# The order of VectorE's layer-norm moments and of its head divisions in the slot loop of a fused two-block transformer kernel

## The chip, the cores and the metric

The kernel runs on one core of a Trainium2 chip. A core has five engines with a queue each, which run side by side and each in its own order: TensorE (PE, matrix products), VectorE (DVE, elementwise work and reductions), ScalarE (ACT, activation functions and copies), GpSimd (POOL, elementwise work) and SyncE (SP, which here only starts transfers). Engines wait for one another, and an engine for itself, by counting semaphores. The metric is the time of one execution on the device in microseconds (us); lower is better.

## The reference, cut to what matters

The input is x, 64 sequences of 64 rows of 256 values, and a context of the same shape. Two blocks follow each other. The first is a decoder layer: self attention, cross attention to the context, and an MLP, each behind a layer norm. The second reads its result as latents: attention over the context and the latents together, then an RMS norm and an MLP.

```python
ln_out = layernorm(hidden_states, ln1_s, ln1_b)
q, k, v = jnp.split(ln_out @ w_qkv + b_qkv, 3, axis=-1)
x = hidden_states + merge_heads(attention(q, k, v, ltor_mask)) @ w_ao + b_ao
ln_out = layernorm(x, ln2_s, ln2_b)
q = ln_out @ w_q + b_q;  k, v = jnp.split(encoder_states @ w_kv + b_kv, 2, axis=-1)
x = x + merge_heads(attention(q, k, v, cross_mask)) @ w_co + b_co
ln_out = layernorm(x, ln3_s, ln3_b)
x = x + gelu(ln_out @ w1 + b1) @ w2 + b2
...
h = jnp.concatenate([context, x], axis=1)         # second block: x are the latents
q = x @ q_w + q_b;  k, v = split(h @ kv_w + kv_b)
a = softmax(where(mask, q @ k.T / DH, -inf)) @ v  # 16 heads of 16
a = a @ out_w + out_b + x
out = rmsnorm(a, postnorm_w)
result = gelu(out @ mlp_w1 + mlp_b1) @ mlp_w2 + mlp_b2 + x
```

A layer norm needs the mean and the variance of each row (the moments). Attention ends with a division of each head by the sum of its exponentials.

## The kernel before

Two sequences make a unit of 128 rows, and there are 32 units. Every unit goes through some 14 stages: self attention (names end in `self`), cross attention (`cross`), the first MLP (`mlp0`), attention of the latents over context and latents (`ctx`, `lat`), and the second MLP (`mlp1`). Products run in halves of f16 (a high and a low part); the parts are made by ACT or POOL (high) and DVE (low), stand in a pair, and are turned by a transfer that SP starts.

The order of the work is written out by hand, once for each engine. A prologue fills the pipeline. A loop over the slots t = 8 to 31 (line 1577 for DVE) then does one stage for each of several units: in slot t the cross attention of unit t-3, the first MLP of t-4, the latent scores of t-5, the latent heads of t-6, the second MLP of t-7 and t-8. An epilogue empties it. The code of a stage is a small function, called with a unit and a name. Its waits are counts of semaphores: `q.wait_ge(name, n)` holds the next instruction of this engine, and all behind it, until the count is n.

The functions that matter, on DVE:

- `moments` (line 1157): BN_STATS reads 256 values of each row into bn (L1165); BN_AGGREGATE makes mean and variance of them in mv (L1167) and waits for the first; then minus_mean and var (L1176, L1177), or for `mlp1` mean_square and var (L1170, L1173), which wait for the second. POOL's `root` (L2448, L2451) waits for var and makes rstd and shift; ACT's `normalize` (L1938) makes xn from them; POOL's `high_pair` (L2457) the high half; DVE's `low_pair` (L1186) the low half; then the transposing transfer and PE's products.
- `denominators` (L1273): the reciprocals over. `divided` (L1280): the heads, from PE's `mix` (L598) in PSUM and over. ACT's `heads_high` (L1952) copies their high half, DVE's `heads_low` (L1195) makes the low half and waits for it.
- `add_residual` (L1291): adds PE's projection (L470) to x or xb; this also sets the PSUM bank free. `masked` (L1231, L1238): the scores (L564) with the mask. `largest_score` (L1248), `largest_both` (L1254), `shifted` (L1267): maxima and the scores less the maximum; for the latents POOL shifts the context's part (L2505).

In ACT's queue a slot has, in this order, `normalize(t-3,"cross")`, `normalize(t-4,"mlp0")`, `values` twice, `heads_high(t-6,"lat")`, `q_bias_cross(t-3)` (L1972), the GELUs (L2017), and the exponentials (L2003).

Of the kernel before, what the change touches and what calls it, by code (L numbers as in the profile page):

```python
# [25 lines left out]
UNITS = B // BU  # L26
# [21 lines left out]
XHAT_UP, TOP = 11, 15  # L48
# [130 lines left out]
def build(nc, x_in, ctxT_in, mask_self_in, mask_cross_in, mask_keys_in, cols_in, rows_in, weights_in,  # L179
          out):  # L180
    with ExitStack() as ctx:
# [842 lines left out]
        def _(e):  # L1024
# [132 lines left out]
            def moments(u, t):  # L1157

                src, shrink = residual(t, u), 2.0 ** (-2 * XHAT_UP)
                steps, n = sem["moments_" + t], 4 * u  # L1160
# [5 lines left out]
                q.wait_ge("moments_" + t, n + 1)  # L1166
                e.bn_aggr(mv[t][:, :], bn[t][:, :]).then_inc(steps, 1)  # L1167
# [142 lines left out]
            moments(0, "self")  # L1310
            moments(1, "self")
            two_heads(0)
# [9 lines left out]
            moments(2, "self")  # L1322
            powers(0, "mid")
# [29 lines left out]
            moments(0, "cross")  # L1353
            bias_rows(0, "co")
            shifted(1, "self", 0)
            shifted(1, "self", 1)
            moments(3, "self")
            k_spread(2, "self", 0)
# [7 lines left out]
            moments(4, "self")  # L1366
            denominators(1, "self")
# [19 lines left out]
            moments(1, "cross")  # L1387
            powers(0, "xin")
# [16 lines left out]
            moments(5, "self")  # L1405
            add_residual(0, "cross")
            moments(0, "mlp0")
            masked(1, "cross", 0)
# [13 lines left out]
            moments(2, "cross")  # L1422
            shifted(1, "cross", 0)
            masked(4, "self", 0)
            moments(6, "self")
            masked(4, "self", 1)
# [26 lines left out]
            moments(1, "mlp0")  # L1453
            largest_score(2, "cross", 1)
# [9 lines left out]
            moments(3, "cross")  # L1464
            k_spread(3, "cross", 0)
# [14 lines left out]
            moments(4, "cross")  # L1480
            hidden_lo(1, "mlp0", 1)
# [19 lines left out]
            moments(2, "mlp0")  # L1501
            largest_score(3, "cross", 1)
# [25 lines left out]
            moments(3, "mlp0")  # L1528
            hidden_lo(2, "mlp0", 0)
            hidden_lo(2, "mlp0", 1)  # L1530
            add_residual(0, "lat")
            moments(0, "mlp1")
            low_pair(3, "mlp0")
# [6 lines left out]
            moments(7, "self")  # L1540
            lat_low(2)
# [1456 lines left out]
```

## Time and profile before

| | |
|---|---|
| time, median of 3 runs | 1089.6 us (1088.24 to 1089.82) |
| span of the profiled execution | 1086.8 us |
| its own time | not listed apart; the median is 2.8 us above its span |
| PE busy | 1004.1 us, 92% |
| DVE busy | 988.4 us, 91% |
| ACT busy | 849.4 us, 78% |
| POOL busy | 681.9 us, 63% |
| mean granted TensorE clock | 0.983 of full speed |

The span is the time from the first to the last instruction. Shares of busy time are averages over prologue, loop and epilogue. An engine's rows stand in the order of its queue, so a row that starts late holds up all behind it. A row of the timeline that waited names the engine that ended its wait in brackets; waits of an engine for itself carry no such note and show only as a later start.

### The profile page before, as it was taken

What the parts mean: (1) busy time and instruction counts of PE and PEld (TensorE: products, weight loads), DVE (VectorE), ACT (ScalarE), POOL (GpSimd) and SP (SyncE); (2) the same over time, 40 slices, a digit from 0 to 9 for tenths busy, and PEclk for the clock granted to TensorE, in tenths of its full rate; (3) what the DMA queues carried; (4) which work ended last, traced back from release to release, by engine and by line L of the source; (5) the groups of instructions that cost most, each with busy time, mean ns of one, the idle gap of its engine ahead of it and who ended that gap; (6) DMA issues with size and microseconds to landing.
All of it is one profiled execution on the core that took longest, in us unless ns stands there. A gap on an engine that the chain in (4) does not pass through costs nothing.

```text
span 1086.8 us, 46478 instructions
## 1 busy us (share of the span) xinstructions
PE 1004.1 (92%) x19180; PEld 890.8 (82%) x19180; DVE 988.4 (91%) x2328; ACT 849.4 (78%) x1905; POOL 681.9 (63%) x909
## 2 busy tenths in 40 slices
PE   6776989999999999999999999999999999998997
PEld 5665778888888888888888888888888888886786
DVE  4989897999999999999999999999999999988763
ACT  3446789887888888888788888878888888786894
POOL 3777575666666667666667676666676676655221
PEclk9879999999999999999999999999999999999999
DMA  8843112222322222222222222222222222311111
GB/s 275 280 114 74 42 39 41 44 45 58 59 49 51 52 57 43 49 54 58 58 49 45 57 47 48 50 58 58 49 49 54 56 44 49 61 37 37 31 37 36
DMA packets 169700, 67.70 MB, mean 62 GB/s; under 512 B 151184, under 2 KB 167312, under 8 KB 168464
## 3 DMA queue, kind: packets, MB, share of 16 engines
q1 hardware_dynamic: 169488, 64.72, 26.1%
q8 instruction: 152, 2.49, 1.0%
q14 instruction: 60, 0.49, 0.2%
HBM read 26.93 MB, written 4.19 MB: 29 GB/s over the span
## 4 chain that ended last, share of the span: by engine, by line
PE 37%; ACT 26%; DVE 20%; issue 11%; POOL 4%; DMA 2%; SPq 0%; ACTq 0%; POOLq 0%; DVEq 0%
PE psum L457 9%; PE psum L598 7%; PE psum L630 7%; ACT staging L2017 7%; PE psum L470 6%; ACT hid_mlp L2017 6%; PE psum L564 3%; ACT L2003 3%; PE psum L584 3%; DVE mx_lat L1248 3%; ACT L2017 2%; ACT probT_self L2003 2%; DVE late L1267 2%; DVE mx_ctx L1254 2%; DMA turned_mlp<-pair_mlp 1%
## 5 line engine op out<-in xcount | busy, mean ns | idle before, releaser
L2499 POOL TENSOR_TENSOR prob_self<-prob_self,add_self 128x512 f32<-128x512 f32 x64 | 86.8, 1376 | 66.1 <-DVE prob_self L1238 63.4
L2499 POOL TENSOR_TENSOR prob_cross<-prob_cross,add_cross 128x512 f32<-128x512 f32 x64 | 94.5, 1495 | 52.9 <-DVE prob_cross L1238 52.9
L2505 POOL TENSOR_TENSOR late<-late,mx_ctx 128x512 f32<-128x512 f32 x64 | 67.3, 1053 | 86.6 <-DVE mx_ctx L1254 84.1
L2017 ACT ACTIVATE hid_mlp<-psum,folded,undo_in 128x128 f32<-128x128 f32 x256 | 95.6, 455 | 6.9 <-PE psum L457 6.4
L2017 ACT ACTIVATE staging<-psum,cols,undo_in 128x128 f32<-128x128 f32 x256 | 97.4, 481 | 3.3 <-PE psum L457 3.1
L457 PE MATMUL psum<-turned_mlp,hi_n 128*128 128x128 f16 x1024 | 94.2, 221 | 1.6 <-DVE late L1267 1.0
L630 PE MATMUL psum<-hi_n,staging 128*128 128x256 f16 x512 | 94.3, 273 | 1.5 <-DVE staging L1297 1.5
L457 PE MATMUL psum<-turned_mlp,hi_m 128*128 128x128 f16 x1024 | 93.4, 220 | 0.6 <-DMA turned_mlp<-pair_mlp 0.5
L630 PE MATMUL psum<-hi_m,parts_mlp 128*128 128x256 f16 x512 | 89.9, 273 | 1.2 <-DVE xb L1291 0.9
L457 PE MATMUL psum<-turned_mlp,lo_n 128*128 128x128 f16 x512 | 90.3, 221 | 0.0
L457 PE MATMUL psum<-turned_mlp,lo_m 128*128 128x128 f16 x512 | 89.6, 220 | 0.0
L457 PEld LDWEIGHTS psum<-turned_mlp,hi_m 128*128 128x128 f16 x1024 | 77.8, 98 | 7.3 <-issue 5.6
L457 PEld LDWEIGHTS psum<-turned_mlp,hi_n 128*128 128x128 f16 x1024 | 78.9, 99 | 4.1 <-issue 1.4
L2448 POOL TENSOR_TENSOR rstd_mlp<-var_mlp,minus_half 128x1 f32<-128x1 f32 x64 | 38.0, 593 | 60.8 <-DVE var_mlp L1173 59.9
L2476 POOL TENSOR_TENSOR xb<-x,rows 128x256 f32<-128x256 f32 x96 | 72.1, 752 | 5.9 <-DVE x L1307 3.0
L2003 ACT ACTIVATE late<-psum 128x512 f32<-128x512 f32 x128 | 69.7, 596 | 6.6 <-PE psum L584 6.4
L630 PE MATMUL psum<-lo_n,staging 128*128 128x256 f16 x256 | 69.8, 273 | 0.0
L630 PE MATMUL psum<-lo_m,parts_mlp 128*128 128x256 f16 x256 | 69.8, 273 | 0.0
L598 PE MATMUL psum<-val_ctx,late 128*64 128x34 f32 x1024 | 62.2, 225 | 0.8 <-ACT late L2003 0.7
L598 PE MATMUL psum<-val_lat,late 128*64 128x34 f32 x1024 | 61.5, 224 | 0.0
L584 PEld LDWEIGHTS psum<-ident,late 64*128 64x128 f32 x1024 | 35.8, 140 | 30.5 <-DVE late L1267 27.4
L584 PE MATMUL psum<-ident,late 64*128 64x64 f32 x1024 | 39.9, 227 | 22.1 <-DVE late L1267 20.7
(265 smaller groups left out, 3850.0 us busy)
## 6 DMA issues: line engine op xcount, KB each, us to landing
xin<-in_x SPq DMA_DIRECT2D x32, 128.0 KB, 2.2
late<-in_ctxT SPq DMA_DIRECT2D x4, 1024.0 KB, 5.7
ctxT<-in_ctxT SPq DMA_DIRECT2D x32, 128.0 KB, 2.0
late<-in_x SPq DMA_DIRECT2D x4, 1024.0 KB, 5.6
out<-xb SPq DMA_DIRECT2D x32, 128.0 KB, 1.9
staging<-in_w_m SPq DMA_DIRECT2D x2, 1024.0 KB, 7.2
staging<-in_w_n SPq DMA_DIRECT2D x2, 1024.0 KB, 5.2
mask<-in_mask_cross SPq DMA_DIRECT2D x32, 32.0 KB, 2.0
```

The lines of the kernel that those rows point to most:

```text
L457: last = e.matmul(out_ap, wt[name][:, k, c:c + P], xs[:, k, :], start=(n == 0), stop=(n == 3 * KH - 1))
L470: last = e.matmul(ps[:, 0:H], xs[:, k, :], wt[name][:, k, c:c + H], start=(n == 0), stop=(n == 3 * KH - 1))
L564: last = e.matmul(ps[here, h * HC * S:(h + 1) * HC * S], qT["lat" if t == "ctx" else t][rows_of, h, here], spread[t][rows_of, h, :, here], ...
L584: last = e.transpose(bank[in_bank["prob_turn", t, a, u]][:, n * S:(n + 1) * S], prob[t][h][here, j * P:(j + 1) * P], ident[here, here])
L598: last = e.matmul(ps[S * a:S * a + S, p * VW:(p + 1) * VW], probT[s][a][:, j, :], val[s][:, a, p, :], start=(n == 0), stop=(n == len(sets) ...
L630: last = e.matmul(ps[:, 0:H], a, wt, start=(g == 0 and n == 0), stop=(g == 1 and n == 11))
L2003: e.activation(probT[t][a][:, :, :], src, ACT.Exp).then_inc(sem["probT_" + t], 1)
L2017: last = e.activation(hid[t][g][:, j * P:(j + 1) * P], ps[:, j * P:(j + 1) * P], ACT.Gelu_apprx_tanh, bias=b1[:, 4 * g + j:4 * g + j + 1], ...
L2448: e.tensor_tensor(rstd[t][:, :], var[t][:, :], minus_half[:, :], ALU.pow).then_inc(sem["rstd_" + t], 1)
L2476: e.tensor_tensor(o[:, :], a[:, :], row, ALU.add).then_inc(sem["plus_bias_" + t], 1)
L2499: e.tensor_tensor(ch, ch, over_heads(a[:, :]), ALU.add).then_inc(sem["added_" + t], 1)
L2505: e.tensor_tensor(ch, ch, over_keys(max_of("ctx", h)), ALU.subtract).then_inc(sem["shifted_ctx"], 1)
```

## The change

`moments` becomes three calls: `moments` (BN_STATS), `aggregate` (BN_AGGREGATE) and `variance` (the rest). In prologue and epilogue the three calls stand one behind the other, so the order there is as before. In the slot loop other calls stand between them. The division of the heads stands one call behind the reciprocals: `largest_score` or `largest_both` goes ahead of it, and for the latent heads both `masked` calls. The statistics have one wait more, for the count of the unit before. The other engines' orders are not touched.

```diff
             def moments(u, t):
-                src, shrink = residual(t, u), 2.0 ** (-2 * XHAT_UP)
-                steps, n = sem["moments_" + t], 4 * u
+                src, steps = residual(t, u), sem["moments_" + t]
+                q.wait_ge("moments_" + t, 4 * u)
...
                 e.bn_stats(bn[t][:, :], src[:, :]).then_inc(steps, 1)
-                q.wait_ge("moments_" + t, n + 1)
-                e.bn_aggr(mv[t][:, :], bn[t][:, :]).then_inc(steps, 1)
+
+            @of_unit
+            def aggregate(u, t):
+
+                q.wait_ge("moments_" + t, 4 * u + 1)
+                e.bn_aggr(mv[t][:, :], bn[t][:, :]).then_inc(sem["moments_" + t], 1)
+
+            @of_unit
+            def variance(u, t):
+
+                shrink, steps, n = 2.0 ** (-2 * XHAT_UP), sem["moments_" + t], 4 * u
                 q.wait_ge("moments_" + t, n + 2)
...
                 moments(t - 7, "mlp1")
                 k_spread(t - 2, "self", 0)
+                aggregate(t - 7, "mlp1")
                 add_residual(t - 3, "self")
+                variance(t - 7, "mlp1")
                 moments(t - 3, "cross")
                 hidden_lo(t - 8, "mlp1", 0)
+                aggregate(t - 3, "cross")
                 add_residual(t - 4, "cross")
+                variance(t - 3, "cross")
                 moments(t - 4, "mlp0")
                 masked(t - 5, "ctx", 0)
+                aggregate(t - 4, "mlp0")
                 low_pair(t - 7, "mlp1")
+                variance(t - 4, "mlp0")
                 low_pair(t - 3, "cross")
...
                 moments(t, "self")
                 k_spread(t - 3, "cross", 0)
+                aggregate(t, "self")
                 denominators(t - 6, "lat")
+                variance(t, "self")
                 masked(t - 2, "self", 0)
+                masked(t - 2, "self", 1)
                 divided(t - 6, "lat")
-                masked(t - 2, "self", 1)
...
                 denominators(t - 2, "self")
+                largest_score(t - 5, "lat", 0)
                 divided(t - 2, "self")
-                largest_score(t - 5, "lat", 0)
                 heads_low(t - 2, "self")
                 denominators(t - 3, "cross")
+                largest_both(t - 5, 0)
                 divided(t - 3, "cross")
-                largest_both(t - 5, 0)
                 largest_score(t - 5, "lat", 1)
```

Three places show what moves on DVE; the line numbers of the changed kernel are 4 to 9 higher. The first is the head of a slot, from the residual of the cross attention (x) on; bn_mlp and mv_mlp are the moments of the first MLP, late the masked scores of the context. Before:

```order
L1291 SCALAR_TENSOR_TENSOR x<-psum,undo,xb 128x256
L1165 BN_STATS bn_mlp<-x 128x6
L1167 BN_AGGR mv_mlp<-bn_mlp 128x2
L1176 TENSOR_SCALAR minus_mean_mlp<-mv_mlp 128x1
L1177 TENSOR_SCALAR var_mlp<-mv_mlp 128x1
L1231 TENSOR_TENSOR late<-psum,keys_mask 128x512
L1183 SCALAR_TENSOR_TENSOR pair_mlp<-xb,rstd_mlp,pair_mlp 128x256
L1186 TENSOR_TENSOR pair_cross<-xn_cross,pair_cross 128x256
```

The same place after the change:

```order
L1300 SCALAR_TENSOR_TENSOR x<-psum,undo,xb 128x256
L1185 TENSOR_SCALAR minus_mean_cross<-mv_cross 128x1
L1186 TENSOR_SCALAR var_cross<-mv_cross 128x1
L1165 BN_STATS bn_mlp<-x 128x6
L1240 TENSOR_TENSOR late<-psum,keys_mask 128x512
L1171 BN_AGGR mv_mlp<-bn_mlp 128x2
L1192 SCALAR_TENSOR_TENSOR pair_mlp<-xb,rstd_mlp,pair_mlp 128x256
L1185 TENSOR_SCALAR minus_mean_mlp<-mv_mlp 128x1
L1186 TENSOR_SCALAR var_mlp<-mv_mlp 128x1
L1195 TENSOR_TENSOR pair_cross<-xn_cross,pair_cross 128x256
```

The last two steps of the cross moments are now behind the residual, and the aggregate of the MLP moments stands behind the mask, its variance behind pair_mlp (the low half of the second MLP).

The second place is the division of the latent heads (heads_lat) in the middle of a slot. Before:

```order
L1273 RECIPROCAL over_lat<-psum 128x16
L1238 TENSOR_TENSOR prob_self<-psum,mask_self 128x512
L1280 TENSOR_TENSOR heads_lat<-psum,over_lat 128x256
L1238 TENSOR_TENSOR prob_self<-psum,mask_self 128x512
L1213 SCALAR_TENSOR_TENSOR spread_cross<-psum,down_of_two_cross,bias_of_two_cross 128x2x128
L1195 TENSOR_TENSOR heads_pair_lat<-heads_lat,heads_pair_lat 128x256
```

The same place after the change:

```order
L1282 RECIPROCAL over_lat<-psum 128x16
L1185 TENSOR_SCALAR minus_mean_self<-mv_self 128x1
L1186 TENSOR_SCALAR var_self<-mv_self 128x1
L1247 TENSOR_TENSOR prob_self<-psum,mask_self 128x512 x2
L1289 TENSOR_TENSOR heads_lat<-psum,over_lat 128x256
L1222 SCALAR_TENSOR_TENSOR spread_cross<-psum,down_of_two_cross,bias_of_two_cross 128x2x128
L1204 TENSOR_TENSOR heads_pair_lat<-heads_lat,heads_pair_lat 128x256
```

Both masked scores (prob_self) and the end of the moments of x stand now ahead of heads_lat.

The third place is the end of a slot, from the reciprocals of the self heads (over_self) on. Before:

```order
L1273 RECIPROCAL over_self<-psum 128x16
L1280 TENSOR_TENSOR heads_self<-psum,over_self 128x256
L1248 TENSOR_REDUCE mx_lat<-psum 128x8
L1195 TENSOR_TENSOR heads_pair_self<-heads_self,heads_pair_self 128x256
L1273 RECIPROCAL over_cross<-psum 128x16
L1280 TENSOR_TENSOR heads_cross<-psum,over_cross 128x256
L1254 TENSOR_TENSOR mx_ctx<-mx_ctx,mx_lat 128x8
L1248 TENSOR_REDUCE mx_lat<-psum 128x8
L1195 TENSOR_TENSOR heads_pair_cross<-heads_cross,heads_pair_cross 128x256
L1254 TENSOR_TENSOR mx_ctx<-mx_ctx,mx_lat 128x8
```

The same place after the change:

```order
L1282 RECIPROCAL over_self<-psum 128x16
L1257 TENSOR_REDUCE mx_lat<-psum 128x8
L1289 TENSOR_TENSOR heads_self<-psum,over_self 128x256
L1204 TENSOR_TENSOR heads_pair_self<-heads_self,heads_pair_self 128x256
L1282 RECIPROCAL over_cross<-psum 128x16
L1263 TENSOR_TENSOR mx_ctx<-mx_ctx,mx_lat 128x8
L1289 TENSOR_TENSOR heads_cross<-psum,over_cross 128x256
L1257 TENSOR_REDUCE mx_lat<-psum 128x8
L1204 TENSOR_TENSOR heads_pair_cross<-heads_cross,heads_pair_cross 128x256
L1263 TENSOR_TENSOR mx_ctx<-mx_ctx,mx_lat 128x8
```

heads_pair_self follows heads_self directly now, and the first mx_ctx follows over_cross directly.

## Rows read from the trace of the kernel before

**Rows 1.** The page, part 1: busy us, share, instructions of each engine.

```profile
PE 1004.1 (92%) x19180; PEld 890.8 (82%) x19180; DVE 988.4 (91%) x2328; ACT 849.4 (78%) x1905; POOL 681.9 (63%) x909
```

**Rows 2.** Timeline of DVE: start us, us, engine, line, op, names; the loop's ends.

```profile
189.21 0.41 DVE L1165 BATCH_NORM_STATS2 bn_mlp<-xb 128x6 f32<-128x256 f32 x1
...
899.06 0.41 DVE L1165 BATCH_NORM_STATS2 bn_mlp<-xb 128x6 f32<-128x256 f32 x1
```

**Rows 3.** Waits, 189 to 899: who for whom, us in total, times, longest.

```profile
PE psum L584 <- DVE late L1267: 18.0, 23, 0.8
```

**Rows 4.** Chain that ended last, 640 to 700: start us, us, what.

```profile
663.12 0.68 PE psum L457 x12
...
663.83 0.02 ACT q_cross L1972
...
664.65 1.28 ACT L2017
...
674.32 1.09 ACT probT_self L2003 x2
...
675.46 1.15 PE psum L598 x32
...
676.63 0.27 DVE over_self L1273
```

**Rows 5.** Timeline of DVE, head of the slot that starts at 652.24.

```profile
652.24 0.41 DVE L1165 BATCH_NORM_STATS2 bn_mlp<-xb 128x6 f32<-128x256 f32 x1
652.69 0.18 DVE L1167 BATCH_NORM_AGGREGATE mv_mlp<-bn_mlp 128x2 f32<-128x6 f32 x1
...
655.69 0.48 DVE L1291 SCALAR_TENSOR_TENSOR x<-psum,undo,xb 128x256 f32<-128x256 f32 x1
...
656.96 0.14 DVE L1177 TENSOR_SCALAR var_mlp<-mv_mlp 128x1 f32<-128x1 f32 x1
657.11 0.69 DVE L1231 TENSOR_TENSOR late<-psum,keys_mask 128x512 f32<-128x512 f32 x1
657.72 0.48 DVE L1183 SCALAR_TENSOR_TENSOR pair_mlp<-xb,rstd_mlp,pair_mlp 128x256 f16<-128x256 f32 x1
...
659.77 0.43 DVE L1186 TENSOR_TENSOR pair_mlp<-xn_mlp,pair_mlp 128x256 f16<-128x256 f32 x1 [0.25 <-POOL pair_mlp L2457]
```

**Rows 6.** Timeline of PE, the same slot.

```profile
655.27 0.38 PE L470 MATMUL psum<-lo_out,heads_turned_cross 128*128 128x256 f16 x2
...
656.32 0.70 PE L564 MATMUL psum<-spread_ctx,q_lat 32*64 32x128 f32 x32
```

**Rows 7.** Timeline of POOL, the same slot.

```profile
657.56 0.55 POOL L2448 TENSOR_TENSOR rstd_mlp<-var_mlp,minus_half 128x1 f32<-128x1 f32 x1
```

**Rows 8.** Timeline of DVE, the division of the latent heads.

```profile
662.68 0.41 DVE L1280 TENSOR_TENSOR heads_lat<-psum,over_lat 128x256 f32<-128x256 f32 x1
```

**Rows 9.** Timeline of ACT, behind that division.

```profile
663.13 0.41 ACT L1952 CAST heads_pair_lat<-heads_lat 128x256 f16<-128x256 f32 x1 [0.92 <-DVE heads_lat L1280]
```

**Rows 10.** Timeline of PE, end of the slot.

```profile
676.52 0.69 PE L564 MATMUL psum<-spread_lat,q_lat 32*64 32x128 f32 x32
```

**Rows 11.** Timeline of DVE, end of the slot.

```profile
677.33 0.69 DVE L1248 TENSOR_REDUCE mx_lat<-psum 128x8 f32<-128x512 f32 x1
...
678.32 0.26 DVE L1273 RECIPROCAL over_cross<-psum 128x16 f32<-128x16 f32 x1
...
678.95 0.16 DVE L1254 TENSOR_TENSOR mx_ctx<-mx_ctx,mx_lat 128x8 f32<-128x8 f32 x1
...
680.43 0.68 DVE L1254 TENSOR_TENSOR mx_ctx<-mx_ctx,mx_lat 128x8 f32<-128x8 f32 x1
...
681.04 1.27 DVE L1267 TENSOR_TENSOR late<-psum,mx_ctx 128x512 f32<-128x512 f32 x2
...
683.02 0.41 DVE L1165 BATCH_NORM_STATS2 bn_mlp<-xb 128x6 f32<-128x256 f32 x1
```

**Rows 12.** Timeline of POOL, end of the slot.

```profile
680.18 0.91 POOL L2476 TENSOR_TENSOR x<-x,rows 128x256 f32<-128x256 f32 x1
```

More of the change, by code:

```diff
@@ L1310, in _ @@
             moments(0, "self")
+            aggregate(0, "self")
+            variance(0, "self")
             moments(1, "self")
+            aggregate(1, "self")
+            variance(1, "self")
             two_heads(0)
@@ L1322, in _ @@
             moments(2, "self")
+            aggregate(2, "self")
+            variance(2, "self")
             powers(0, "mid")
@@ L1353, in _ @@
             moments(0, "cross")
+            aggregate(0, "cross")
+            variance(0, "cross")
             bias_rows(0, "co")
@@ L1357, in _ @@
             moments(3, "self")
+            aggregate(3, "self")
+            variance(3, "self")
             k_spread(2, "self", 0)
@@ L1366, in _ @@
             moments(4, "self")
+            aggregate(4, "self")
+            variance(4, "self")
             denominators(1, "self")
@@ L1387, in _ @@
             moments(1, "cross")
+            aggregate(1, "cross")
+            variance(1, "cross")
             powers(0, "xin")
@@ L1405, in _ @@
             moments(5, "self")
+            aggregate(5, "self")
+            variance(5, "self")
             add_residual(0, "cross")
             moments(0, "mlp0")
+            aggregate(0, "mlp0")
+            variance(0, "mlp0")
             masked(1, "cross", 0)
@@ L1422, in _ @@
             moments(2, "cross")
+            aggregate(2, "cross")
+            variance(2, "cross")
             shifted(1, "cross", 0)
@@ L1425, in _ @@
             moments(6, "self")
+            aggregate(6, "self")
+            variance(6, "self")
             masked(4, "self", 1)
@@ L1453, in _ @@
             moments(1, "mlp0")
+            aggregate(1, "mlp0")
+            variance(1, "mlp0")
             largest_score(2, "cross", 1)
@@ L1464, in _ @@
             moments(3, "cross")
+            aggregate(3, "cross")
+            variance(3, "cross")
             k_spread(3, "cross", 0)
@@ L1480, in _ @@
             moments(4, "cross")
+            aggregate(4, "cross")
+            variance(4, "cross")
             hidden_lo(1, "mlp0", 1)
@@ L1501, in _ @@
             moments(2, "mlp0")
+            aggregate(2, "mlp0")
+            variance(2, "mlp0")
             largest_score(3, "cross", 1)
@@ L1528, in _ @@
             moments(3, "mlp0")
+            aggregate(3, "mlp0")
+            variance(3, "mlp0")
             hidden_lo(2, "mlp0", 0)
@@ L1532, in _ @@
             moments(0, "mlp1")
+            aggregate(0, "mlp1")
+            variance(0, "mlp1")
             low_pair(3, "mlp0")
@@ L1540, in _ @@
             moments(7, "self")
+            aggregate(7, "self")
+            variance(7, "self")
             lat_low(2)
@@ L1642, in _ @@
             moments(UNITS - 3, "cross")
+            aggregate(UNITS - 3, "cross")
+            variance(UNITS - 3, "cross")
             add_residual(UNITS - 4, "cross")
@@ L1704, in _ @@
             moments(UNITS - 2, "cross")
+            aggregate(UNITS - 2, "cross")
+            variance(UNITS - 2, "cross")
             add_residual(UNITS - 3, "cross")
@@ L1749, in _ @@
             moments(UNITS - 1, "cross")
+            aggregate(UNITS - 1, "cross")
+            variance(UNITS - 1, "cross")
             k_spread(UNITS - 1, "cross", 0)
@@ L1793, in _ @@
             moments(UNITS - 1, "mlp0")
+            aggregate(UNITS - 1, "mlp0")
+            variance(UNITS - 1, "mlp0")
             add_mlp(UNITS - 6, "mlp1")
```

20 lines of the change are left out of this document (added).

## The prediction

> **What bounds the kernel now.** The page's busy line comes first: PE 92% and DVE 91% of the span, so neither has room by itself [rows 1]. The timeline then gives the slot's length. The loop's 24 slots each begin at DVE's statistics of the block xb; the first starts at 189.21, the last at 899.06, so a slot lasts (899.06 - 189.21) / 23 = 30.86 us, and 24 of them are 741 us of the 1086.8 [rows 2]. The waits say who waits in the loop: PE waits for DVE's second shift of the latent scores, 18.0 us in 23 slots, 0.78 us in each [rows 3]. The chain that ended last says where one slot's length comes from [rows 4]. PE works from that shift up to the query product of the cross attention (until 663.12 + 0.68 = 663.80). ACT takes it up at 663.83 and is then never idle: table load at 664.65, GELUs, second table load, exponentials of the self scores from 674.32. PE's mix starts at 675.46, DVE's reciprocal at 676.63, and DVE carries the chain to the next shift (from 681.04 [rows 11]). So a slot is three pieces: PE up to 663.80, ACT up to the mix, DVE's tail. Time counts only if it moves one of them.
>
> **What the change takes away, and why I price it at nothing.** The statistics take 0.41, but the aggregate that waits for them starts 0.45 later [rows 5]. A row that waits for nothing starts 0.08 before the one ahead of it ends (the mask at 657.11 takes 0.69, the next row starts at 657.72) [rows 5]. A self-wait thus costs 0.45 - 0.33 = 0.12, that behind the aggregate about as much. Four moments lose two each, two divisions one each: about 10 x 0.12 = 1.2 us of DVE a slot. At the head of the slot, however, DVE soon waits for others. Its add of the cross residual at 655.69 follows PE's projection, which ends at 655.27 + 0.38 = 655.65; the mask at 657.11 follows PE's scores, which wait for that add and end at 656.32 + 0.70 = 657.02 [rows 5, 6]. Neither can start earlier because DVE arrives earlier. The saving becomes idle time there, and the same fixed points now stand between the pieces of the moments.
>
> The Trainium skill bears on this: "VectorE: DVE Perf Modes", section The DRAIN you can't avoid, says in my words that a semaphore between two chained VectorE operations costs nothing extra. The trace disagrees for these short ones (0.45 against 0.33). By that rule the saving would be zero instead of 1.2 us a slot; my sum is the same by both.
>
> **What it moves: the head of the slot.** DVE's variance of the MLP block ends now at 656.96 + 0.14 = 657.10 [rows 5]. After the change the statistics stand ahead of the mask, but the aggregate behind it, and the variance behind the low half of the other MLP block. From the fixed mask at 657.11: aggregate 657.72, low half 0.18 - 0.08 later at 657.82, minus_mean 0.48 - 0.08 later at 658.22, variance 0.07 later at 658.29, end 658.43. That is 1.33 us later. Behind it hangs a chain over three engines: POOL's root, ACT's normalisation, POOL's high half, DVE's low half at 659.77, for which DVE already waits 0.25 us now; there is no slack to swallow anything [rows 5]. POOL's root starts today at 657.56, when POOL comes free [rows 7]; afterwards at 658.43 + 0.04 = 658.47, so 0.91 later. The chain from it to DVE's low half is 659.77 - 657.56 = 2.21 as before: low half at 660.68. DVE has nothing else it may do (its rows are in order) and idles.
>
> Then the division of the latent heads. Today it starts 662.68 - 659.77 = 2.91 behind the low half [rows 5, 8]. Now both masks stand ahead of it instead of one (+0.60, the distance 657.72 - 657.11), and two self-waits of the moments of x are gone (-0.23): 660.68 + 2.91 + 0.37 = 663.96. ACT's copy of the heads stands in ACT's queue ahead of the bias of the cross queries; today it starts 0.04 behind the division (662.68 + 0.41 = 663.09 against 663.13) and ends at 663.54, in time for 663.83 [rows 4, 8, 9]. Afterwards it ends at 663.96 + 0.41 + 0.04 + 0.41 = 664.82, so the bias starts at 664.84 instead of 663.83: +1.01 us. Everything behind it on ACT is back to back, so the mix and DVE's reciprocal come 1.01 later too. PE has its own delay of about 0.9 from the transposed low half, which stays beneath this; nothing else on POOL or SP is moved.
>
> **What it moves: the tail.** I count from the reciprocal of the self heads, R = 676.63. The reduction of the latent scores is now ahead of the division, but its scores leave PE at 676.52 + 0.69 = 677.21 = R + 0.58 [rows 10], so it starts at R + 0.62, hardly ahead of today's 677.33 = R + 0.70 [rows 11]. Division at R + 1.23, end 0.42 later at R + 1.65. Behind the division now stands directly the low half of the self heads, which needs ACT's copy (0.04 + 0.41, as in [rows 9]): R + 2.10, start R + 2.13. Until now the reduction covered that copy. The reciprocal of the cross heads follows 0.33 later at R + 2.46; today it is at 678.32 = R + 1.69, so 0.77 are lost. Part comes back: the maximum of both (mx_ctx) now stands directly behind that reciprocal, 0.17 instead of 678.95 - 678.32 = 0.63. It starts at R + 2.63 against R + 2.32: +0.31. From it to the shift I keep today's 681.04 - 678.95 = 2.09, because that stretch is set by POOL: the second maximum takes 0.68 where the first takes 0.16, and ends (681.11) with POOL's 0.91 us row at 681.09 [rows 11, 12], which is started by the first maximum through the row ahead of it. Tail: +0.31.
>
> The Trainium skill, "SBUF — State Buffer", section SBUF: two separate sides, says that VectorE and GpSimd take a shared port pair as an exclusive lock, whoever starts first holding it for the whole instruction. The 0.68 against 0.16 agrees. By it the tail keeps its 2.09; without it the stretch would shrink by up to 0.52, and the tail would be -0.21 instead of +0.31.
>
> **Sum.** 1.01 + 0.31 = 1.32 us on the slot shown, which lasts 683.02 - 652.24 = 30.78 [rows 5, 11]: 32.10. Against the mean of 30.86 that is +1.24, as the short waits that make some slots longer are covered by the new one; 24 x 1.24 = 29.8. Prologue and epilogue keep their order (the three calls stand together there) and get 0. The profiled execution spans 1086.8, and the median of the runs is 1089.6, 2.8 more for what lies around it. 1086.8 + 29.8 + 2.8 = 1119.4 us.
>
> Bounds. The head is at least the extra mask, 0.60 (the low half as today), less the 0.29 that ACT's copy has to spare (663.83 - 663.54): 0.3. It is at most 1.5, if POOL's later root meets DVE rows that stretch it as they do the maximum (0.52). I take 1.01, since its points are rows. The tail is at least -0.21 and at most 0.77, if nothing comes back. All ends together would give 24 x 0.1 to 24 x 2.2; for the range I take half of each side's way, since the ends of the two terms don't hang together.
>
> **The rivals.** (1) DVE is the engine that bounds, and its 1.2 us a slot reach PE's 0.78 us of waiting [rows 3]: 24 x 0.78 = 18.7 faster, 1070.9. For it: the 91%. It decides once the head's variance comes no later than POOL can use it, that is by 657.56; against it stand 1.33 us of lateness where DVE waits already. Chance 0.07. (2) The self-waits were beneath other engines' time and the delays are covered as well: 1089.6. Chance 0.03. (3) The low half is not late, because the mask at 657.11 comes earlier than I think, and only the tail's 0.31 counts: 24 x 0.31 = 7.4, 1097.0. Against it: PE's scores, which wait for the add. Chance 0.10. (4) Both terms at their long ends (+1.5 and +0.77), against it that POOL has pauses between: 24 x 2.2 = 53, up to 1142. Chance 0.08.
>
> **How the numbers follow.** My forecast, 1119.4, has 0.72. The range 1096 to 1131 takes in (3) and the halves of the bounds, and leaves out (1), (2) and most of (4), somewhat under 0.2 together. A difference of 0.2% (2.2 us) is about what a measurement of this kernel can tell from none. Faster 0.07, same 0.04 (case 2 and a weak tail), slower 0.89.
>
> **What would show it.** In the profile after: a slot of about 32.1 us; DVE idle about 1 us before pair_mlp<-xn_mlp with POOL as releaser; ACT's q_cross no longer released by PE but starting right behind heads_pair_lat, whose wait for DVE heads_lat grows; a new wait of some 0.5 us of DVE heads_pair_self for ACT; POOL's two rows at the end as long as before; PE's waits grow in the middle of the slot (hidden or k_lat products), not only at the transposes of the latent scores. I would be wrong if DVE's idle before pair_mlp stays at 0.25 us, if q_cross is still released by PE, or if the slot gets shorter than 30.8.

## The result

| | before | after |
|---|---|---|
| median | 1089.7 us | 1130.6 us |
| its runs | 1088.24 to 1090.49 | 1128.95 to 1132.33 |
| profiled span | 1086.8 us | 1127.5 us |
| slot, mean of the loop | 30.86 us | 32.48 us |

The ratio is 1.0373, 95% interval 1.0355 to 1.0392: the changed kernel is 3.7% slower, 40.8 us. The forecast was 1119.4 us in a range of 1096 to 1131; the measured median lies 0.4 us inside its upper end. Of the 40.7 us between the spans, the loop holds 24 x (32.48 - 30.86) = 38.9.

### The profile page after: what moved, and what is told of

It reads as the page before. It is cut to its first block, busy times and chain, and to the rows that moved or that the text cites. A ratio compares the mean times of both kernels' runs of the same rounds, so it can differ in the third digit from the quotient of the medians.

```text
span 1127.5 us, 46602 instructions
## 1 busy us (share of the span) xinstructions
PE 1017.8 (90%) x19180; PEld 891.0 (79%) x19180; DVE 984.2 (87%) x2328; ACT 854.8 (76%) x1905; POOL 675.4 (60%) x909
## 4 chain that ended last, share of the span: by engine, by line
PE 42%; DVE 25%; issue 15%; ACT 11%; POOL 7%; DMA 1%; ACTq 0%; POOLq 0%; SPq 0%; DVEq 0%
PE psum L457 16%; PE psum L630 7%; PE psum L584 6%; PE psum L470 4%; PE psum L564 4%; PE psum L598 3%; DVE late L1276 2%; DVE mx_self L1257 2%; DVE staging L1306 2%; DVE prob_self L1247 2%; DVE mx_ctx L1263 2%; ACT xn_mlp L2019 1%; POOL rstd_mlp L2529 1%; DVE mx_lat L1257 1%; ACT xn_cross L2019 1%
## 5 line engine op out<-in xcount | busy, mean ns | idle before, releaser
L2580 POOL TENSOR_TENSOR prob_self<-prob_self,add_self 128x512 f32<-128x512 f32 x64 | 82.0, 1300 | 60.6 <-DVE prob_self L1247 57.8
L598 PE MATMUL psum<-val_ctx,late 128*64 128x34 f32 x1024 | 62.2, 225 | 0.7 <-ACT late L2084 0.6
L598 PE MATMUL psum<-val_lat,late 128*64 128x34 f32 x1024 | 61.6, 224 | 0.0
L630 PEld LDWEIGHTS psum<-hi_n,staging 128*128 128x128 f16 x512 | 50.0, 98 | 12.5 <-issue 4.5
L630 PEld LDWEIGHTS psum<-hi_m,parts_mlp 128*128 128x128 f16 x512 | 50.1, 98 | 11.8 <-DVE parts_mlp L1306 6.1
```

The costliest lines, as they stand in the source:

```text
L598: last = e.matmul(ps[S * a:S * a + S, p * VW:(p + 1) * VW], probT[s][a][:, j, :], val[s][:, a, p, :], start=(n == 0), stop=(n == len(sets) ...
L630: last = e.matmul(ps[:, 0:H], a, wt, start=(g == 0 and n == 0), stop=(g == 1 and n == 11))
L2580: e.tensor_tensor(ch, ch, over_heads(a[:, :]), ALU.add).then_inc(sem["added_" + t], 1)
```

## The profile after

The busy line, against [rows 1]. Each engine does about as much as before in a longer span; no busy time explains 40 us.

```profile
PE 1017.8 (90%) x19180; PEld 891.0 (79%) x19180; DVE 984.2 (87%) x2328; ACT 854.8 (76%) x1905; POOL 675.4 (60%) x909
```

The loop's ends on DVE, against [rows 2]: (936.23 - 189.18) / 23 = 32.48 us.

```profile
189.18 0.41 DVE L1165 BATCH_NORM_STATS2 bn_mlp<-xb 128x6 f32<-128x256 f32 x1
...
936.23 0.41 DVE L1165 BATCH_NORM_STATS2 bn_mlp<-xb 128x6 f32<-128x256 f32 x1
```

The waits of PE and DVE over the whole span that matter here (engine, what waits, for whom: us in total, times, longest). The first, fourth, fifth and last are new. The second stood at 20.7 in 27 over the whole span before, of which [rows 3] show the loop's part.

```profile
PE psum L564 <- DVE xb L1316: 18.2, 24, 0.8
...
PE psum L584 <- DVE late L1276: 15.1, 27, 1.0
DVE pair_mlp L1195 <- POOL pair_mlp L2538: 14.6, 27, 1.7
...
DVE mx_lat L1257 <- PE psum L564: 11.6, 27, 0.8
DVE heads_pair_self L1204 <- ACT heads_pair_self L2033: 11.3, 24, 0.5
PE psum L564 <- ACT val_ctx L2076: 11.0, 24, 0.6
```

PE now waits with two of its scores (L564) in each of the 24 slots, once for ACT's val_ctx and once for DVE's add of the MLP product (L1316). By the kernel's bank numbers each of the two reads a PSUM bank that those scores are then written into. Times below are also given from the slot's start, here 643.76.

DVE's timeline, head of that slot; it answers to [rows 5, 8].

```profile
643.76 0.41 DVE L1165 BATCH_NORM_STATS2 bn_mlp<-xb 128x6 f32<-128x256 f32 x1
...
648.63 0.69 DVE L1240 TENSOR_TENSOR late<-psum,keys_mask 128x512 f32<-128x512 f32 x1 [0.41 <-PE psum L564]
...
649.76 0.14 DVE L1186 TENSOR_SCALAR var_mlp<-mv_mlp 128x1 f32<-128x1 f32 x1
...
652.01 0.42 DVE L1195 TENSOR_TENSOR pair_mlp<-xn_mlp,pair_mlp 128x256 f16<-128x256 f32 x1 [0.52 <-POOL pair_mlp L2538]
...
655.26 0.42 DVE L1289 TENSOR_TENSOR heads_lat<-psum,over_lat 128x256 f32<-128x256 f32 x1
...
656.15 1.47 DVE L1204 TENSOR_TENSOR heads_pair_lat<-heads_lat,heads_pair_lat 128x256 f16<-128x256 f32 x1
...
658.14 0.47 DVE L1316 SCALAR_TENSOR_TENSOR xb<-psum,undo_out,x 128x256 f32<-128x256 f32 x1
```

The mask stands at 4.87, as before (657.11 - 652.24), waiting 0.41 for PE. The variance is at 6.00 instead of 4.72, the low half at 8.25 instead of 7.53, the division at 11.50 instead of 10.44. Then a row that nobody had in view: heads_pair_lat takes 1.47 us. In the kernel before the same row takes 0.41:

```profile
664.00 0.41 DVE L1195 TENSOR_TENSOR heads_pair_lat<-heads_lat,heads_pair_lat 128x256 f16<-128x256 f32 x1
```

POOL's timeline, first before, then after. Two rows of prob_self stand in one line of 2.70 or 2.50 us.

```profile
662.85 2.70 POOL L2499 TENSOR_TENSOR prob_self<-prob_self,add_self 128x512 f32<-128x512 f32 x2 [2.34 <-DVE prob_self L1238]
```

```profile
647.89 0.55 POOL L2529 TENSOR_TENSOR rstd_cross<-var_cross,minus_half 128x1 f32<-128x1 f32 x1 [1.24 <-DVE var_cross L1186]
...
649.47 0.56 POOL L2538 CAST pair_cross<-xn_cross 128x256 f16<-128x256 f32 x1 [0.76 <-ACT xn_cross L2019]
650.00 0.54 POOL L2529 TENSOR_TENSOR rstd_mlp<-var_mlp,minus_half 128x1 f32<-128x1 f32 x1
650.62 0.19 POOL L2532 TENSOR_TENSOR shift_mlp<-minus_mean_mlp,rstd_mlp 128x1 f32<-128x1 f32 x1
...
654.84 2.50 POOL L2580 TENSOR_TENSOR prob_self<-prob_self,add_self 128x512 f32<-128x512 f32 x2 [2.10 <-DVE prob_self L1247]
```

Before, heads_pair_lat begins 1.15 us into POOL's pair (664.00 - 662.85), ahead of the second row. After, it begins 1.31 us in (656.15 - 654.84), when POOL, at half of its 2.50 us, has just begun its second; it ends at 657.62, and POOL's pair ends at 657.34. The DVE row is held until POOL's is done. Before, POOL's first row, of 1.28 us, had 0.13 left when the DVE row began, and the DVE row ended 0.29 behind it; after, the second row had 1.19 left, and the DVE row ended 0.28 behind it. So in both kernels it ends about 0.28 behind the POOL row that runs when it begins, and 1.19 + 0.28 makes the 1.47.

ACT's timeline, against [rows 9] and the q_cross of [rows 4].

```profile
650.91 0.60 ACT L2019 ACTIVATE xn_mlp<-x,shift_mlp,rstd_mlp 128x256 f32<-128x256 f32 x1 [1.50 <-POOL shift_mlp L2532]
651.42 1.50 ACT L2076 ACTIVATE val_ctx<-psum,undo 64x128 f32<-64x128 f32 x4
...
655.71 0.40 ACT L2033 CAST heads_pair_lat<-heads_lat 128x256 f16<-128x256 f32 x1 [1.27 <-DVE heads_lat L1289]
656.14 0.81 ACT L2053 ACTIVATE q_cross<-psum,folded,down_q 128x128 f32<-128x128 f32 x2
```

The query bias q_cross follows ACT's copy without a wait and starts at 12.38 instead of 11.59, so 0.79 later. PE's two rows of scores are later by 0.52 and by 1.51. First the rows before, at 8.77 and 13.49 of their slot (start 652.24), then after, at 9.29 and 15.00:

```profile
661.01 0.69 PE L564 MATMUL psum<-spread_self,q_self 32*64 32x128 f32 x32
...
665.73 0.69 PE L564 MATMUL psum<-spread_cross,q_cross 32*64 32x128 f32 x32
```

```profile
653.05 0.89 PE L564 MATMUL psum<-spread_self,q_self 32*64 32x128 f32 x32 [0.46 <-ACT val_ctx L2076]
...
658.76 0.70 PE L564 MATMUL psum<-spread_cross,q_cross 32*64 32x128 f32 x32 [0.45 <-DVE xb L1316]
```

The chain of waits in this slot (start, us, what) runs through the held row. The 1.36 us stand as "issue", since no semaphore explains them; read beside POOL's line they are the hold.

```profile
655.71 0.41 ACT heads_pair_lat L2033
...
656.15 0.04 DVE heads_pair_lat L1204
656.19 1.36 issue
657.55 0.67 DVE mx_self L1257
658.22 0.40 DVE xb L1316
...
658.76 0.70 PE psum L564 x32
659.45 2.79 PE psum L457 x48
...
668.33 1.12 PE psum L598 x32
669.45 0.71 PE psum L564 x32
```

From the cross scores on the chain is PE's own work, up to the mix of the self heads (L598) that ends at 669.45, just ahead of DVE's reciprocal at 669.50. In the loop PE's idle time between these scores and that reciprocal has a median of 0.21 us a slot before, a wait for ACT's probT_self ahead of the mix, and of 0.00 after. So the middle piece of the slot, which ACT bounded before, is bounded by PE here: the reciprocal follows the cross scores by 10.74 us, against 10.90 before.

The tail on DVE, against [rows 11]; R, the start of the reciprocal of the self heads, is 669.50.

```profile
669.50 0.26 DVE L1282 RECIPROCAL over_self<-psum 128x16 f32<-128x16 f32 x1
670.18 0.69 DVE L1257 TENSOR_REDUCE mx_lat<-psum 128x8 f32<-128x512 f32 x1 [0.42 <-PE psum L564]
...
671.67 0.42 DVE L1204 TENSOR_TENSOR heads_pair_self<-heads_self,heads_pair_self 128x256 f16<-128x256 f32 x1 [0.47 <-ACT heads_pair_self L2033]
...
672.18 0.10 DVE L1263 TENSOR_TENSOR mx_ctx<-mx_ctx,mx_lat 128x8 f32<-128x8 f32 x1
...
674.23 1.27 DVE L1276 TENSOR_TENSOR late<-psum,mx_ctx 128x512 f32<-128x512 f32 x2
```

From R to the shift 674.23 - 669.50 = 4.73 us, against 4.41. POOL's row beneath the end, against [rows 12], is as long as it was:

```profile
673.37 0.91 POOL L2557 TENSOR_TENSOR x<-x,rows 128x256 f32<-128x256 f32 x1
```

## The experiments

The theory: the time comes from three places, and each can be taken back alone. (M) The spread moments make POOL's roots, ACT's mlp0 normalisation and so val_ctx late, and PE's self scores wait. (L) The lat division behind both masks puts heads_pair_lat beneath POOL's second prob_self row. (T) The tail is 0.32 longer. The rivals: the added semaphore wait itself costs; or ACT's q_cross alone carries the head; or the parts don't add.

The first seven columns of numbers are medians over 21 slots of the loop, from each kernel's timeline, in us: from the slot's start the low half (pair_mlp), PE's self scores, heads_pair_lat (with its own duration), PE's cross scores, R; then the way from R to the shift. The last is the mean slot.

| kernel | pair_mlp | self scores | heads_pair_lat | takes | cross scores | R | R to shift | slot |
|---|---|---|---|---|---|---|---|---|
| before | 7.53 | 8.77 | 11.76 | 0.42 | 13.49 | 24.39 | 4.41 | 30.85 |
| after | 8.24 | 9.29 | 12.39 | 1.47 | 14.99 | 25.73 | 4.73 | 32.46 |
| a_wait_only | 7.58 | 8.83 | 11.81 | 0.41 | 13.55 | 24.44 | 4.40 | 30.86 |
| b_divisions_only | 7.53 | 8.77 | 11.92 | 1.46 | 14.52 | 25.26 | 4.72 | 31.98 |
| c_moments_only | 8.24 | 9.29 | 12.22 | 0.41 | 14.02 | 24.91 | 4.40 | 31.39 |
| d_lat_division_back | 8.25 | 9.29 | 12.23 | 0.42 | 14.02 | 24.91 | 4.73 | 31.70 |
| f_low_half_later | 8.24 | 9.29 | 13.77 | 0.41 | 14.09 | 25.31 | 4.61 | 31.93 |
| h_self_division_back | 8.25 | 9.29 | 12.39 | 1.46 | 14.99 | 25.73 | 3.90 | 31.66 |
| g_maximum_first | 7.53 | 8.77 | 11.75 | 0.42 | 13.49 | 24.39 | 3.90 | 30.36 |
| m_values_first | 9.50 | 8.77 | 13.48 | 0.41 | 15.16 | 26.05 | 4.41 | 32.45 |
| n_one_group_back | 8.18 | 9.23 | 12.16 | 0.42 | 13.95 | 24.86 | 4.40 | 31.37 |
| p_one_group_only | 8.40 | 9.45 | 12.63 | 0.42 | 14.32 | 25.22 | 4.40 | 31.68 |
| q_both_orders | 8.18 | 9.22 | 12.16 | 0.42 | 13.95 | 24.85 | 3.89 | 30.83 |
| r_two_groups_back | 7.72 | 8.96 | 11.70 | 0.41 | 13.68 | 24.71 | 3.77 | 30.50 |

**a_wait_only.** The new functions with their wait, nothing between the calls, divisions as before.

```diff
+                aggregate(t - 4, "mlp0")
+                variance(t - 4, "mlp0")
                 masked(t - 5, "ctx", 0)
```

> The moments are split into three calls that stand one behind the other everywhere, the divisions stand as before; what is left of the change is the one wait more on each statistics row. Theory M (the change costs by what it moves, nothing by its waits): within 0.2% of before, 1089.6. Rival W (the added wait costs sequencer time on each of 4 statistics a slot, up to 0.05 us each in the chain): 24 x 0.2 = 5 us slower, 1094.5.

Measured 1090.8 us, ratio 1.001 (0.9994 to 1.0027). The added wait costs nothing that can be measured; all of the 3.7% is order.

**b_divisions_only and c_moments_only.** Each half of the change alone.

```diff
                 masked(t - 2, "self", 0)
-                divided(t - 6, "lat")
                 masked(t - 2, "self", 1)
+                divided(t - 6, "lat")
```

> Only the three divisions are moved; the moments stay together as before. Theory L (DVE's low half of the latent heads, a row with two SBUF inputs, now starts just behind POOL's second row of the self scores and is held for its length): heads_pair_lat takes about 1.47 us instead of 0.42, the score of the cross attention starts about 1.05 us later, the tail costs 0.2 to 0.3: slot +1.2, 1118. Rival H (no such hold; only ACT's copy is 0.33 late and the tail 0.31): heads_pair_lat 0.42 us, slot +0.64, 1105. Rival M1 (the cost sits in the moments alone): 1090.

> Only the moments are spread in the loop; the three divisions stand as before. The low half of the first MLP comes 0.7 us later, the division of the latent heads then about 0.5 us later (10.93 us into the slot instead of 10.44), one self-wait group being saved; ACT's bias of the cross queries +0.2 to +0.3. Theory L: heads_pair_lat starts just ahead of POOL's second row as before and takes 0.42: slot +0.3, 1097. Rival (the moments carry the whole head term by themselves): slot +0.8 to +1.0, 1109 to 1114.

Measured: divisions 1115.9 us, ratio 1.0237 (1.0207 to 1.0267); moments 1103.3 us, ratio 1.0125 (1.0087 to 1.0164), against 1089.6 for the kernel before. They add within these intervals: 26.3 + 13.7 = 40.0 of 40.8. The time of the divisions was 2 us under what was expected. That of the moments fell between the theory's 1097 and the rival's 1109: they cost 0.54 us a slot where 0.3 was expected, because PE's late self scores were not in the theory. The long heads_pair_lat comes with the divisions (1.46) and not with the moments (0.41):

```profile
650.28 1.46 DVE L1195 TENSOR_TENSOR heads_pair_lat<-heads_lat,heads_pair_lat 128x256 f16<-128x256 f32 x1
```

```profile
671.43 0.41 DVE L1204 TENSOR_TENSOR heads_pair_lat<-heads_lat,heads_pair_lat 128x256 f16<-128x256 f32 x1
```

The delays of PE's scores split alike: self scores +0.52 from the moments and 0 from the divisions, cross scores +0.53 and +1.03, which makes 1.56 against the 1.50 seen together. In c the chain of waits runs from the late variance of cross over POOL's cast and its root of mlp0, ACT's normalisation and val_ctx to PE's self scores and on to q_cross, which comes 0.52 later (12.11 against 11.59), as R does. Its step from ACT to PE (start, us, what; slot start 659.21):

```profile
667.98 0.38 ACT val_ctx L2076
...
668.50 0.70 PE psum L564 x32
```

**d_lat_division_back.** The kernel after, with the lat division between the masks again (the reverse of the diff above).

> The changed kernel with only the division of the latent heads back between the two masks. Theory L: heads_pair_lat goes back to 0.42 us, PE's cross scores stop waiting for DVE's add; what is left is the moments' part (13.7 us measured alone) and the tail's 0.16 to 0.3 a slot: 1107 to 1111. Rival (the division of the latent heads is a small part, under 5 us of the 26 that the divisions cost together): 1125 or more.

Measured 1111.1 us, ratio 1.0202 (1.0186 to 1.0218): 19.5 us back, at the upper edge of what was expected. The row takes 0.42, the cross scores come at 14.02 as with the moments alone, and the wait for L1316 is gone.

**f_low_half_later.** The kernel after, with the low half of the lat heads behind three rows, so that it starts when POOL has finished its pair.

```diff
-                heads_low(t - 6, "lat")
                 largest_score(t - 2, "self", 0)
                 add_mlp(t - 8, "mlp1")
                 k_spread(t - 5, "lat", 0)
+                heads_low(t - 6, "lat")
```

> The changed kernel with heads_low of the latent heads moved three calls later, behind largest_score, add_mlp and k_spread, so that DVE doesn't meet POOL's row with it and add_mlp frees its PSUM bank earlier. Theory L: add_mlp no longer waits behind the held row, PE's cross scores start about 0.5 to 1 us earlier and the slot is bound by ACT's late copy (+0.8) and the tail (+0.25): slot 31.9, 1115. Rival (the hold is only a symptom; the slot is set by ACT's copy and the tail anyway): no change against the changed kernel, 1130.

Measured 1117.2 us, ratio 1.0262 (1.0213 to 1.031): 13.4 us back. The same row, later still, takes 0.41, so it is the meeting with POOL's row that makes it long. The cross scores return to 14.09, and ACT bounds the middle piece again. R keeps 0.40 more than in d, and the traces say why (medians). ACT's q_cross follows the late copy without a wait, at 12.38 against 12.12 in d, and PE's mix waits 0.42 for ACT's exponentials instead of 0.22 and starts at 24.02 instead of 23.74: 0.28. The other 0.12 is another held row: DVE's pair_lat, just ahead of the reciprocal, begins as POOL passes from one row to the next (xb to ctx_lo, in the median slot 0.04 behind it) and takes 0.99, ending 0.28 behind POOL's row; in d it takes 0.47.

**h_self_division_back.** The kernel after, with the self division ahead of the reduction again.

```diff
+                divided(t - 2, "self")
                 largest_score(t - 5, "lat", 0)
-                divided(t - 2, "self")
```

> The changed kernel with the division of the self heads back ahead of the reduction of the latent scores, so that this covers ACT's copy again. Theory T: heads_pair_self loses its wait of 0.47 us and mx_lat its wait of 0.42; the shift comes 0.75 to 0.87 earlier: 1110 to 1112. Rival (the slot is set by the head alone and the tail's wait is idle time anyway): 1130.5.

Measured 1109.4 us, ratio 1.0187 (1.017 to 1.0204). That is 0.6 us under the range. The head is untouched (R at 25.73), the tail falls from 4.73 to 3.90. So the tail's +0.32 is a loss of 0.83 by the self division and a gain of 0.51 by the cross division.

**g_maximum_first.** The kernel before, with only the edit that gains.

```diff
-                divided(t - 3, "cross")
                 largest_both(t - 5, 0)
+                divided(t - 3, "cross")
```

> The kernel before with one swap: largest_both (mx_ctx) directly behind the reciprocals of the cross heads, ahead of their division; nothing else of the change. Theory T (the stretch from the first mx_ctx to the shift is set by POOL's rows and only moves with its start): mx_ctx starts 0.46 us earlier, the shift too, slot 30.4, 24 x 0.46 = 11 us faster, 1078.6. Rival P (PE is not free for the transposes earlier, or the shift doesn't follow): within 0.2% of before, 1089.6.

Measured 1078.0 us, ratio 0.9898 (0.9877 to 0.9919): faster than both kernels, by one move out of the changed kernel's seven. DVE's tail, then POOL's:

```profile
670.99 0.10 DVE L1254 TENSOR_TENSOR mx_ctx<-mx_ctx,mx_lat 128x8 f32<-128x8 f32 x1
...
672.05 0.45 DVE L1195 TENSOR_TENSOR heads_pair_cross<-heads_cross,heads_pair_cross 128x256 f16<-128x256 f32 x1
```

```profile
671.18 1.04 POOL L2505 TENSOR_TENSOR late<-late,mx_ctx 128x512 f32<-128x512 f32 x1 [1.08 <-DVE mx_ctx L1254]
```

The maximum releases POOL's late row 0.50 us earlier (26.44 of the slot against 26.94 before, medians), and that row is nearly over when heads_pair_cross starts, which takes 0.45. In c_moments_only, whose tail is that of before, it takes 0.88 beneath the same POOL row.

**m_values_first.** c_moments_only, with ACT's val_ctx ahead of the mlp0 normalisation, to free PE's bank early.

```diff
+                values(t - 5, "ctx")
                 normalize(t - 4, "mlp0")
-                values(t - 5, "ctx")
```

> Moments spread, divisions as before (the kernel that took 1103.3), and in ACT's queue the values of the context ahead of the normalisation for the first MLP. Theory V (the moments cost through PE: its self scores wait for a PSUM bank that ACT's val_ctx frees, and val_ctx stands in ACT's queue behind the late xn_mlp): the wait of 0.46 us before the self scores goes, slot 31.0, 1092 to 1095. Rival C (the cost comes over ACT's copy of the latent heads or over the transposed low half): no change, 1103.

A miss: 1129.1 us, ratio 1.0366 (1.0348 to 1.0385). The waits of its whole span:

```profile
DVE pair_mlp L1195 <- POOL pair_mlp L2538: 44.7, 27, 1.8
...
PE psum L630 <- DVE staging L1306: 30.0, 27, 1.2
ACT val_ctx L2076 <- PE psum L598: 29.2, 24, 1.2
```

PE's self scores are on time (8.77). But val_ctx itself waits 1.2 us for PE's mix, and the normalisation stood behind it in ACT's queue: the low half comes at 9.50, DVE idles 1.8 us, and PE waits 1.2 us for the staging behind it. So this run shows that the bank can be freed in time, and that the low half then takes over; it does not by itself show what the bank's wait costs in c. For that stand c's chain of waits and run r below.

**n_one_group_back and p_one_group_only.** Which of the four spread moments costs: c with mlp0's calls together again, and a with only mlp0's spread.

```diff
                 moments(t - 4, "mlp0")
-                masked(t - 5, "ctx", 0)
                 aggregate(t - 4, "mlp0")
-                low_pair(t - 7, "mlp1")
                 variance(t - 4, "mlp0")
+                masked(t - 5, "ctx", 0)
+                low_pair(t - 7, "mlp1")
```

> The moments of three residuals stay spread over the slot (mlp1, cross, self); only those of mlp0, whose result the path through GpSimd waits for, stand together again ahead of masked(ctx, 0). Divisions as in the kernel before. Theory: the whole cost of the spread moments is that mlp0's variance comes 1.3 us later and DVE's pair_mlp with it; with these together pair_mlp starts no later than before and the slot is back at 30.9 us or a little under: 1082 to 1091 us. Rival: the spread costs wherever it is made (x of self waits for PE, ACT's normalizations come late): 1096 to 1103 us, near the kernel in which all four are spread.

> The complement: the three calls follow each other directly for self, cross and mlp1, and only mlp0's are spread, over masked(ctx, 0) and the low half of mlp1. Divisions as in the kernel before. Theory: pair_mlp about 0.7 us later, at offset 8.2 to 8.5 us of the slot, nothing saved elsewhere: 1101 to 1108 us, as the kernel with all four spread or slower by the self-waits that it does not save. Rival: no more than 1095 us, since the cost lies in the other groups.

Measured 1103.7 us, ratio 1.0118 (1.0095 to 1.014), and 1111.2 us, ratio 1.0189 (1.0163 to 1.0216). The first expectation fell: with mlp0's variance back at 4.8, nothing is won. The second came out 3 us above its range of 1101 to 1108, and 8 us above c. So once mlp0's variance is late, spreading the other three groups as well wins 0.29 us a slot (31.39 against 31.68); by what was not taken apart. POOL's rows of n (slot start 629.95), then of p (633.54):

```profile
634.09 0.55 POOL L2529 TENSOR_TENSOR rstd_cross<-var_cross,minus_half 128x1 f32<-128x1 f32 x1 [1.23 <-DVE var_cross L1186]
...
635.67 0.50 POOL L2538 CAST pair_cross<-xn_cross 128x256 f16<-128x256 f32 x1 [0.76 <-ACT xn_cross L2019]
636.13 0.55 POOL L2529 TENSOR_TENSOR rstd_mlp<-var_mlp,minus_half 128x1 f32<-128x1 f32 x1
```

```profile
639.83 0.66 POOL L2529 TENSOR_TENSOR rstd_mlp<-var_mlp,minus_half 128x1 f32<-128x1 f32 x1 [0.85 <-DVE var_mlp L1186]
```

In n the mlp0 root waits for nobody: it stands behind POOL's cast for cross, which is late because the variance of cross came at 3.91 instead of 2.72. It starts at 6.18. In p it waits for mlp0's variance and starts at 6.29. Before it starts at 5.32. Two delays meet in one queue, and either is enough.

**q_both_orders and r_two_groups_back.** g with the moments spread as in n; then cross's calls together too, so that only those of mlp1 and self are spread.

```diff
                 moments(t - 3, "cross")
-                hidden_lo(t - 8, "mlp1", 0)
                 aggregate(t - 3, "cross")
-                add_residual(t - 4, "cross")
                 variance(t - 3, "cross")
+                hidden_lo(t - 8, "mlp1", 0)
+                add_residual(t - 4, "cross")
```

> The order that the findings point to: the moments of mlp1, cross and self spread, mlp0's together, and the first largest-score call ahead of the division of cross, the other two divisions as in the kernel before. Theory: the gain of the maximum first (11.7 us) and that of the spread (0 to 8 us) add: 1070 to 1079 us. Rival: TensorE bounds both and VectorE's saved time is worth nothing: 1078 us.

> As the kernel in which both orders are changed (maximum first; moments of mlp1, cross and self spread; 1088.8 us), but cross's three calls stand together again too, so that only mlp1's and self's are spread. Reading of the last three traces: GpSimd takes the root of cross, its cast and the root of mlp0 in one row, and either variance late (cross at 3.93 instead of 2.74, or mlp0 at 6.02 instead of 4.74) makes it late by the same 0.7 us, so putting one back gave nothing. Theory: with both back, mlp0's normalization on ScalarE starts at 6.4 to 6.6 instead of 7.1, TensorE's self scores wait under 0.2 us for val_ctx, and the time is that of the maximum first alone or less, by the self-waits saved: 1072 to 1080 us. Rival: the wait of add_residual(self) for TensorE (0.58 us at offset 1.5) or mlp1's root 1.2 us later costs by itself: 1084 to 1089 us.

Measured 1088.8 us, ratio 0.9995 (0.998 to 1.001), and 1082.8 us, ratio 0.9949 (0.993 to 0.9968). The first was wrong for n's reason. The second confirms the path but missed its range by 3 us: ACT's normalisation starts at 6.62 (6.43 before), the self scores at 8.96 without a wait. Along g, r, q the self scores stand at 8.77, 8.96, 9.22 and the slot at 30.36, 30.50, 30.83. The 0.19 of the self scores comes from the cross statistics, which start 0.21 later (2.18 against 1.97): the last two rows of mlp1's moments now stand between the add of the self residual and them. R comes 0.32 later than in g, as pair_lat is held here too (0.99 in 16 of 21 slots); its 0.13 is made up in the tail (3.77 against 3.90). Against the kernel before, no spreading of the moments gained time; g is the fastest kernel that was run.

## Why the prediction was right in kind and short in size

- **The saving priced at nothing.** Right. The next row starts 0.33 behind the slot's first statistics instead of 0.45, so a self-wait does cost 0.12, and what is saved becomes idle time: 0.41 before the mask at the same offset 4.87.
- **The head's first link, the low half.** Said at offset 8.44, measured 8.24 (median) and 8.25 (the slot shown). The variance at 6.00 and POOL's root at 6.24 came where they were put (6.05 and 6.23). The 0.2 came back on POOL: shift_mlp takes 0.19 where it took 0.39. But the argument was too narrow: it followed mlp0's variance alone. Cross's late variance alone gives 6.18 (n), so mlp0's was not the one that decided.
- **The division.** Said at 11.72, measured 11.50, the same 0.2.
- **The head's last link is the step that failed.** "ACT's copy, then the bias of the cross queries: +1.01", everything else beneath. The bias came 0.79 later. What PE waited for was elsewhere: its self scores for val_ctx (+0.52, the moments' share) and its cross scores for DVE's MLP add (+1.50), because heads_pair_lat was held 1.05 us longer by POOL. From the cross scores on PE worked without a pause up to R, so ACT's late bias was covered. At R the head is 25.73 - 24.39 = +1.34, not +1.01. The path that was predicted exists: in f, where the row is not held, PE's mix waits for ACT and starts 0.80 later than before (24.02 against 23.22). The prediction had the shared port in its tail and in its upper bound (1.5, with the roots stretched), but did not lay the moved rows of the head against POOL's rows. That PE's own delay stays beneath ACT's was wrong.
- **The tail.** Said 4.41 to 4.72, measured 4.73; the reduction R + 0.68 (said 0.62), the maximum of both R + 2.68 (said 2.63), the wait for ACT 0.47 (said about 0.5). By h and g it is +0.83 and -0.51.
- **The Trainium skill, "SBUF — State Buffer", section SBUF: two separate sides**, says that a VectorE instruction with two SBUF inputs and a GpSimd instruction that reads SBUF share a port pair as an exclusive lock, which the first to start holds for the whole instruction. The runs agree in the head, where the prediction did not apply it: 1.47 us beneath POOL's row, 0.42 and 0.41 when moved to either side of it (d, f), and before, where DVE's row came first, POOL's second row took 1.47 instead of 1.28.
- **The sum.** Head +1.34 and tail +0.32 less 0.05 at the slot's end make the 1.61 of the table, against 1.24 predicted: 24 x 0.37 = 9 us of the 11 us missing. The other 2 lie outside the loop or in rounding. The range held the result narrowly, and by luck more than by its reasoning: two of the four runs lie above 1131. Its lower end does not follow from the rule that it states either; half of the way from 24 x 1.24 down to 24 x 0.1 us gives 1105.7, not 1096.
- **The signs.** The wait of heads_pair_self, q_cross behind the copy, POOL's rows and a slot above 32 came as told. DVE's idle before pair_mlp came as 0.52, not 1. PE's new waits stand in the middle of the slot, at the scores and not at the hidden or k_lat products.
- **The rivals.** The bound by DVE (1070.9) and no change fell with b and c, in which each half of the change is slower by itself. Only the tail (1097.0) fell too: the head costs four times as much. "Both long ends" (up to 1142) named the mechanism, rows of DVE and POOL that stretch each other, but for POOL's root and not for heads_pair_lat; of its two ends the head came near (1.34 of 1.5) and the tail did not (0.32 of 0.77).

What stays open: why PE's self scores take up to 0.99 us instead of 0.69 in 5 of 21 slots in which they have waited (0.89 in the one shown), and what the spreading of the other groups wins in c against p.

## What to carry to other kernels

When rows move in an in-order engine, lay them over the other engines' rows at their new times as well as along their own chain: a row of 0.4 us that came 0.16 us later against another engine's long row became one of 1.5. Follow every chain that enters the same queue, since two delays that meet there hide each other: undoing one alone (n) gave nothing. Take a reordering apart edit by edit: here one move out of a change that cost 3.7% was worth 1.0% by itself.

## What the runs showed of the hardware

- A DVE tensor_tensor with two SBUF inputs, 128x256, takes 0.41 us alone. In the meetings read here, begun beneath a POOL tensor_tensor of 128x512, it ends 0.28 to 0.29 behind POOL's row, whatever is left of that row: 0.13 left gives 0.41 (heads_pair_lat before), 0.17 gives 0.45 (heads_pair_cross in g), 0.60 gives 0.88 (heads_pair_cross before), 1.19 gives 1.47 (heads_pair_lat after). Each of these is the same in all 21 slots to 0.01. In the trace the hold has no releaser; the chain calls it issue.
- DVE's tensor_reduce of 128x512 from SBUF (mx_self, mx_cross) was not seen to stretch: 0.67 to 0.69 in all 246 rows that began beneath a POOL row, before and after together.
- Where POOL passes from one row to the next just as a DVE row with two SBUF inputs begins, a few hundredths decide. In r, pair_lat takes 0.99 where POOL's next row (ctx_lo) begins up to 0.05 us behind it, and 0.48 where that begins 0.06 behind.
- The wait goes both ways. POOL's 128x1 root of cross takes 0.99 us in 20 of 21 slots before, where it begins 0.16 behind DVE's staging row and ends 0.41 behind it. In the one slot where the two begin within 0.01 it takes 0.55, as it does after, where the staging row is over before it.
- An added semaphore wait that is already met costs nothing to be seen (ratio 1.001 for four more a slot), while one that waits for the row just ahead costs 0.12.
